# ScalarE issues the loads of step sizes and inputs for the next slot, instead of the sync engine

## What is computed

```
dA   = exp(dt[d,l] * A[d,n])                       # the "decay"
h[n] = h[n] * dA + (dt[d,l] * u[d,l]) * B[n,l]     # the scan
y[d,l] = sum over n of h[n] * C[n,l]  +  D[d] * u[d,l]
x1   = x + swapaxes(y * silu(z))                   # z: layernorm of x
x2   = x1 + experts(layernorm(x1))                 # 16 routed, 1 shared
```

## Time and profile before

| | |
|---|---|
| runs | 1041.66 us median of 3 (1039.03 to 1046.57) |
| profiled execution, own time | 1043.07 us |
| span of its profile | 1041.0 us |
| mean granted TensorE clock | 0.927 |
| busy: PE, DVE, ACT, POOL | 899.0, 822.7, 530.3, 748.0 us |
| transfers of `m_dt` and of `m_u` | 16 each, 256 KB each |
| slots in which the moved waits stand | 14 (numbers 1 to 14) |

### The profile page before, as it was taken

The page is one execution under the profiler, slowest core; times in us unless marked ns, Lnnn a source line. Parts: engine busy times, 40 slices in busy tenths (PEclk is TensorE's granted clock), DMA queues, the critical chain, the costliest instruction groups (busy, mean ns, idle before and its releaser), DMA issues.

```text
span 1041.0 us, 16655 instructions
## 1 busy us (share of the span) xinstructions
PE 899.0 (86%) x4352; PEld 653.8 (63%) x4353; DVE 822.7 (79%) x1347; ACT 530.3 (51%) x995; POOL 748.0 (72%) x466
## 2 busy tenths in 40 slices
PE   5876656678999889989999999889999899998994
PEld 2322334555666556656666555659989799897993
DVE  4788899999999799989999616866898979898000
ACT  3777734456665566646665222124554455454541
POOL 2435889889999799989993101038889688787873
PEclk9986555899999999999999989989999999999997
DMA  5567912563228422563210310154777667684443
GB/s 174 194 269 286 369 39 90 201 230 92 75 70 311 153 81 81 202 232 91 81 60 31 133 73 11 65 169 112 211 190 211 181 183 221 159 238 99 79 61 41
DMA packets 69987, 152.14 MB, mean 146 GB/s; under 512 B 7585, under 2 KB 23969, under 8 KB 64306
## 3 DMA queue, kind: packets, MB, share of 16 engines
q1 hardware_dynamic: 59410, 126.97, 35.4%
q0 software_dynamic: 10528, 24.65, 12.5%
HBM read 112.80 MB, written 38.80 MB: 146 GB/s over the span
## 4 chain that ended last, share of the span: by engine, by line
PE 40%; DVE 31%; issue 17%; DMA 4%; ACT 3%; POOL 2%; DVEq 1%; SPq 0%; ACTq 0%; POOLq 0%
DVE bank L1365 8%; PE bank L667 7%; PE bank L771 6%; PE bank L773 6%; PE bank L772 6%; DVE gs L1379 6%; PE bank L686 5%; PE bank L613 3%; DVE p_acc L1307 2%; DVE e_gu_lo L1528 2%; DVE e_gu_hi L1527 2%; PE bank L575 2%; DVE bank L1520 1%; DVE h_p L1365 1%; DMA xt<-x_scratch 1%
## 5 line engine op out<-in xcount | busy, mean ns | idle before, releaser
L1175 POOL TENSOR_TENSOR dbu<-bcs,m_w 128x2048 f32<-128x2048 f32 x64 | 294.8, 4608 | 12.0 <-DVE bank L1365 9.2
L927 ACT ACTIVATE bank<-m_dt,c_a 128x512 f32<-128x512 f32 x256 | 171.7, 686 | 176.4 <-DVE gs L1379 176.3
L1365 DVE TENSOR_TENSOR_SCAN bank<-bank,dbu 128x512 f32<-128x512 f32 x192 | 229.8, 1215 | 16.9 <-ACT bank L927 8.0
L667 PE MATMUL bank<-ws_gu,f_xnT 128*128 128x352 f32 x576 | 192.2, 475 | 3.3 <-ACT f_hT L949 2.9
L613 PE MATMUL bank<-ident,gs 128*128 128x128 f32 x768 | 134.7, 306 | 63.5 <-DVE gs L1379 54.5
L613 PEld LDWEIGHTS bank<-ident,gs 128*128 128x128 f32 x768 | 96.3, 155 | 122.4 <-DVE gs L1379 100.3
L667 PEld LDWEIGHTS bank<-ws_gu,f_xnT 128*128 128x128 f32 x576 | 106.7, 197 | 50.5 <-issue 5.2
L771 PE MATMUL bank<-e_gu_hi,e_xT_hi 128*128 x376 | 129.9, 346 | 7.7 <-POOL e_xT_lo L1237 5.9
L1379 DVE TENSOR_TENSOR gs<-bank,bcs 128x512 f32<-128x512 f32 x192 | 127.0, 668 | 0.0
L773 PE MATMUL bank<-e_gu_hi,e_xT_lo 128*128 x376 | 122.0, 324 | 0.0
L772 PE MATMUL bank<-e_gu_lo,e_xT_hi 128*128 x376 | 121.8, 324 | 0.0
(11 more groups left out here) (172 smaller groups left out, 1689.2 us busy)
## 6 DMA issues: line engine op xcount, KB each, us to landing
bcs<-bc_scratch SPq DMA_DIRECT2D x32, 1024.0 KB, 9.0
e_gu<-in_wgu SPq DMA_DIRECT2D x16, 1408.0 KB
e_dn<-in_wdn SPq DMA_DIRECT2D x16, 512.0 KB
out_rows<-xt SPq DMA_DIRECT2D x18, 256.0 KB, 2.1
p_x<-in_x SPq DMA_DIRECT2D x4, 1024.0 KB, 7.1
u_scratch<-p_u SPq DMA_DIRECT2D x4, 1024.0 KB, 3.9
silu_z_scratch<-p_sz SPq DMA_DIRECT2D x4, 1024.0 KB, 5.3
dt_scratch<-p_dt SPq DMA_DIRECT2D x4, 1024.0 KB, 4.1
```

The source lines that it names most:

```text
L667: last = mm(dst[:, 0:I], lhs[t], ws_gu[:, t, off:off + I], start=t == 0, stop=t == KH - 1)
L927: f(HS[k % RING_H][:], m_dt[:, q % 2, :], ACT.Exp, scale=c_a[:, q, n:n + 1]).then_inc(exp_done, 1)
L1175: g.tensor_tensor(part_, Bs[:, gr * GRP:(gr + 1) * GRP, :], w, ALU.mult).then_inc(dbu_ready, 1)
L1365: v.tensor_tensor_scan(to, h, dbu[:, n, :], 0.0, ALU.mult, ALU.add).then_inc(scan_done, 1)
```

## The change

ACT gets a function `operands` that does the waits of SP and issues both loads. It is called behind the second decay (`OPERANDS_AT = 1`) of every slot but the first and the last. The wait for `exp_done` stands ahead of the load of `m_dt`, those for `w_ready` and `du_ready` ahead of the load of `m_u`, each followed by an increment of a semaphore that nobody waits for (`held`). In slot 3 ACT also waits for the stores of `u` and `dt`. SP's waits and loads at the head of its slot are gone. Since the last slot has no load, ACT's batch 3 is written out: its loop now covers batches 1 and 2.

```diff
+OPERANDS_AT = 1
...
@@ SP, slot
-                if more:
-                    sp.wait_ge(exp_done, i * NS)
-                    sp.wait_ge(w_ready, i)
-                    sp.wait_ge(du_ready, i)
-                    held(sp)
-                    load_dtu(nb, nq)
...
@@ ScalarE
+            def operands(b, q, i):
+
+                par = q % 2
+                act.wait_ge(exp_done, i * NS)
+                held(act)
+                nc.scalar.dma_start(m_dt[:, par, :], dt_d[bass.ds(b, 1), :, q, :].rearrange("a p l -> p (a l)")).then_inc(d_loaded[par], 16)
+                act.wait_ge(w_ready, i)
+                held(act)
+                act.wait_ge(du_ready, i)
+                held(act)
+                nc.scalar.dma_start(m_u[:, par, :], u_d[bass.ds(b, 1), :, q, :].rearrange("a p l -> p (a l)")).then_inc(u_loaded[par], 16)
...
-            def slot(b, q, rows):
+            def slot(b, q, rows, last=False):
...
                 for n in range(NS):
                     decay(b, q, n)
+                    if n == OPERANDS_AT and not first and not (last and q == DT - 1):
+                        if isinstance(b, int) and b == 0 and q == DT - 1:
+                            act.wait_ge(u_stored, 16 * B)
+                            act.wait_ge(dt_stored, 16 * B)
+                        operands(*((b, q + 1) if q < DT - 1 else (b + 1, 0)), b * DT + q)
...
-            with act.Fori(1, B) as b:
+            with act.Fori(1, B - 1) as b:
                 for q in range(DT):
                     slot(b, q, True)
+            for q in range(DT):
+                slot(B - 1, q, True, last=True)
```

## The result

The changed kernel takes 1044.8 us in the median (22 runs, 1038.66 to 1050.66), the kernel before 1041.76 (22 runs, 1036.74 to 1046.57). The ratio is 1.0038, with an interval of 1.0021 to 1.0055: 2 to 6 us slower, some 4 by the ratio and 3.0 by the medians, within 1%. The profiled execution has an own time of 1046.89 us and a span of 1044.8.

A forecast was written before the change was run, and what follows sets the result against it. VectorE was taken to set the pace of the scan stage. Terms of 0 + 0 + 1.4 + 0 us on the median of 1041.66 gave 1043.1 us; own range 1041 to 1046, 8 in 10 for 1036 to 1049.5.

The forecast's parts named there:

- rival 4: Slots 7 and 11: queues take turns, `m_w` 4 us late, 2.5 us lost twice, 1046.7 us in all; chance 0.15.
- the two signs: Wrong if VectorE idles in ordinary slots (issues dearer than 1.49 us), or batch-change idle moves by more than a microsecond.
- What bounds it: Scan stage: VectorE, busy 27.30 of 27.30 us in slots 6 and 7, sets the pace; batch-change idle is its jump.
- Part 1: SP's queue: two issues fewer free 1.28 us, `B` starts some 1.7 us earlier in slots 7 and 11; worth 0.
- Part 2: ScalarE, between second and third decay: both issues add 0.6 to 1.3 us, taken as 0.7; cost 0 in all slots.
- The threshold of 1.49 us: ScalarE's decay behind the `f_hT` copies: VectorE notices only added time over 0.58 + 0.91 = 1.49 us.
- Part 3, first slots of a batch: Loads come some 4 us sooner past `C`; idle before `m_w` in slots 8 and 12 shrinks 3 us or more; gain 0.
- Part 3, slots 7 and 11: Loads share with `B`: `m_w` 0.3 us earlier to 4.1 later; 0.7 us lost, twice, 1.4 us.
- turn by turn: Slots 7 and 11: 2 KB rows alternate with 8 KB, loads get a fifth, `m_w` 4.1 us late, 2.5 us lost.
- What the change doesn't touch: VectorE's jump at the change of batch, idle 5.02 and 3.77 us, was taken to stay as it was.
- Part 4: ScalarE's written-out batch 3: one jump back saved, longer loop body, both covered by VectorE's jump; 0.

The follow-up runs named there:

- experiment 8: The kernel before with VectorE's loop over batches 1 to 3 written out, so without its jump: 1032.07 us, ratio 0.9936.
- experiment 2: The changed kernel, but SP again issues the loads for the first slot of a batch, ahead of `B`; ScalarE issues the others: 1041.54 us, ratio 1.0014.
- experiment 6: The changed kernel with SP waiting for both loads before issuing `B`, and each of ScalarE's loads in two pieces of 64 rows: 1055.11 us, ratio 1.0131.
- experiment 3: The changed kernel, but ScalarE issues the loads only in slots 3, 7 and 11, SP in all others: 1040.14 us, ratio 1.0014.
- experiment 10: The changed kernel with VectorE's loop written out, so without its jump: 1043.44 us, ratio 1.0039 to the kernel before.
- experiment 12: The kernel before, with two of the four `C` loads issued only after VectorE's first scan of the next batch: 1042.62 us, ratio 1.0030.
- experiment 4: The kernel before with nothing but ScalarE's batch 3 written out, all loads staying with SP: 1044.09 us, ratio 1.0028.

## Why the prediction held, point by point

The number was 1043.1 us, with 1044.8 measured against a median of before that is now 1041.76: 1.4 us forecast, 3 to 4 found. "Within 1%" was right. But the case that came true is the slower rival 4, not the forecast, and by one of the two signs that the prediction set for being wrong, the idle at a change of batch, it was wrong.

- **What bounds it** held: VectorE sets the pace, its ordinary slots kept their 27.28 us. That the wait in the earlier trace rows named after GpSimd is VectorE's jump is shown by experiment 8.
- **Part 1** held: SP's lost issues gain nothing, and `B` starts 1.6 us sooner in the slot (1.7 predicted). SP goes on to the store of `x1` in 11 of the 14 slots, not in 13: in slots 3, 7 and 11 it is `B` that follows.
- **Part 2** held: 0.7 us taken, 0.71 measured in slot 6 (0.65 of idle where two decays overlapped by 0.06; 0.36 in the written-out batch 3), cost 0 (experiment 2). The threshold of 1.49 us held, at 1.56 (experiment 6). The price of going beyond it lacked a term: where TensorE's granted clock falls after its stop, 1.2 us per slot come on top, in slot 14 even with the scans in time.
- **Part 3, first slots of a batch**: in slot 8 `m_u` landed after 4.6 us instead of 8.0, and nothing was gained, as said. At the next change it took 9.1 us where it was 7.0, and the idle before `m_w` there grew from 4.44 to 4.85 us instead of shrinking by 3 or more, so it isn't sooner every time.
- **Part 3, slots 7 and 11** is the step that was mis-sized: "I take 0.7 us, twice". The bound "turn by turn" (`m_w` 4.1 us late, 2.5 us of VectorE) was the right one: 4.8 and 4.7 us late, 3.2 and 4.6 us of VectorE. Taking half of the price of a 3.0 us delay had no row behind it. The way from the delay to the loss held: the second `g_p` behind `m_w`, less the slack of 0.71 us on TensorE and of 0.91 at the second `f_h`. In slot 11 the first of the two is 0.23 us in the kernel before:

```profile
442.95 1.26 POOL L1191 TENSOR_TENSOR g_p<-h_p,bcs 128x512 f32<-128x512 f32 x1
```

```profile
444.44 0.60 PE L613 MATMUL bank<-ident,g_p 128*128 128x128 f32 x4
```

| us | second `g_p` late by | less 1.62 (slot 7) or 1.14 (slot 11) | VectorE's idle at both `f_h` |
|---|---|---|---|
| change, slot 7 | 4.81 | 3.19 | 3.23 |
| change, slot 11 | 4.68 | 3.54 | 4.61 |
| experiment 3, slot 7 | 5.14 | 3.52 | 3.55 |
| experiment 3, slot 11 | 4.25 | 3.11 | 3.14 |
| experiment 10, slot 7 | 5.22 | 3.60 | 3.62 |
| experiment 10, slot 11 | 4.74 | 3.60 | 3.63 |

Five of six fit within 0.04 us; the sixth is TensorE's clock (last section). Only the place was wrong: most of the idle comes at the first `f_h` already, because the first `g_p` behind `m_w` stops TensorE too.

- **What the change doesn't touch**: "the change doesn't touch that jump" failed. It fell by 2.63 and 1.35 us, more than the microsecond that was set as the mark of a wrong prediction, and gave half of the loss back. Late by its stop, VectorE jumped when fewer bytes were in flight, and the packet of its instructions came 0.8 us after its last instruction had started instead of 3.7; that the bytes are the reason experiment 12 bears out in part. Experiment 10, in which there is no jump, shows the whole price: 7.1 us.
- **Part 4** held in the scan stage (experiment 4).

So the total came out near the forecast because two errors stood against each other, 7.8 us instead of 1.4 and 4.0 us back instead of none. That is luck, not the working.

## What to carry to other kernels

A small load on a queue of its own passes the transfers that stood ahead of it, but it now shares with the transfers that used to stand behind it. If those have larger rows, it gets its share by packets and not by bytes: look at what is issued within the time that the load takes to land (up to 9.9 us here), and make the rows alike or hold the bulk back. And before pricing a delay, look for an idle of fixed place just behind it (a jump, a late load): the delay can be paid from there, and will show in full once that idle is removed. Where the delay stops TensorE, ask also whether its clock falls: that adds to the price.

## What was not expected of the hardware

TensorE's clock. After its stop for `g_p` in slot 11 it worked for 5.6 us, to 447.0, at a granted clock of 0.50. Busy time by stretch in the changed kernel (columns as in the earlier trace rows), then the lines of TensorE:

```profile
437.50:441.40 3.90, 0.50 (x2) 0.00 (x0) 3.90 (x6) 3.27 (x7) 2.50 (x3) 0.86 1.00 415
441.40:443.00 1.60, 1.51 (x6) 1.27 (x7) 1.60 (x3) 0.69 (x1) 1.60 (x2) 0.50 0.53 165
...
445.00:447.00 2.00, 2.00 (x6) 1.16 (x5) 0.00 (x0) 1.18 (x2) 2.00 (x3) 0.50 1.02 287
```

```profile
441.49 1.12 PE L608 MATMUL bank<-ident,g_p 128*128 128x128 f32 x4 [3.48 <-POOL g_p L1205]
442.39 2.55 PE L662 MATMUL bank<-ws_gu,f_xnT 128*128 128x352 f32 x4
...
447.66 1.35 PE L662 MATMUL bank<-ws_gu,f_xnT 128*128 128x352 f32 x4
```

0.50 is the lower level, 1.2 GHz. The piece that takes 1.35 us at 2.4 GHz took 2.55. So slot 11 cost 4.61 us, 1.07 more than the late `g_p` accounts for: the first `f_sg` was done at 445.95 + 0.95 = 446.9, and VectorE waited for TensorE's piece until 449.0. In slot 7 the clock was down for some 3 us only (from about 324.4). There the sum is what the second `g_p` sets (3.19 us of 3.23): against slot 11 of experiment 3, where the clock stayed up, more of it only falls to the first `f_h`. In experiment 10 the clock was up again by about 445 in slot 11, and the sum is 3.63 us, as in its slot 7. In slot 11 of experiment 3 it stayed at 1.00 after a stop of 3.03 us. What decides between these is not shown. In the kernel before the granted clock is 1.00 in both slots.

And an issue on ScalarE takes 0.34 us for 128 rows but about 0.5 for 64, and 0.35 to 0.38 for 32 (medians of `m_dt` and `m_u`): cutting a load into pieces makes none of them cheaper to issue.
